# Streamed units of a second cross-attention: loads of turned weights placed behind other stores, query weights split earlier, two borders reordered

## The reference, cut to what matters

```python
q = (text_hidden @ Wq).reshape(B, T_text, N_HEADS, HEAD_DIM).transpose(0, 2, 1, 3)
...
scores = jnp.einsum('bhtd,bhsd->bhts', q, k) / scale
scores = jnp.where(mask, scores, -jnp.inf)
attn = jax.nn.softmax(scores, axis=-1)
out = jnp.einsum('bhts,bhsd->bhtd', attn, v)
out = out.transpose(0, 2, 1, 3).reshape(B, T_text, N_HEADS * HEAD_DIM)
return out @ Wo
```

## Time and profile before

| what | value |
|---|---|
| median of three runs | 2262.18 us |
| the profiled execution's own time | 2273.13 us |
| its span | 2271.1 us |
| TensorE busy | 2167.3 us, 95% |
| VectorE busy | 1467.5 us, 65% |
| ScalarE busy | 1051.5 us, 46% |
| GpSimd busy | 773.7 us, 34% |
| mean granted TensorE clock | 0.985 |
| streamed units, first to last turn | 878.6 to 1614.6 us |

### The profile page before, as it was taken

The page is one execution under the profiler, slowest core; times in us unless marked ns, Lnnn a source line. Parts: engine busy times, 40 slices in busy tenths (PEclk is TensorE's granted clock), DMA queues, the critical chain, the costliest instruction groups (busy, mean ns, idle before and its releaser), DMA issues. The chain is left out here.

```text
span 2271.1 us, 32392 instructions
## 1 busy us (share of the span) xinstructions
PE 2167.3 (95%) x10153; PEld 1764.7 (78%) x10153; DVE 1467.5 (65%) x2989; ACT 1051.5 (46%) x1895; POOL 773.7 (34%) x705
## 2 busy tenths in 40 slices
PE   8999999999999998898999999898899999999999
PEld 6778788889999876676777767676677888888887
DVE  7864365546777685677777777777677555555544
ACT  5532210114665665666666666666564323323221
POOL 4423445521111262444545445554332202121000
PEclk9999999999999999999999999999999999999999
DMA  6422221116778694666666666666402233232331
GB/s 225 137 99 68 77 60 33 33 63 249 277 262 291 224 314 157 194 187 186 197 190 194 194 192 194 194 203 194 139 1 84 84 97 103 100 128 72 109 116 52
DMA packets 250573, 339.17 MB, mean 149 GB/s; under 512 B 22048, under 2 KB 159776, under 8 KB 247648
## 3 DMA queue, kind: packets, MB, share of 16 engines
q1 hardware_dynamic: 242224, 310.75, 41.9%
q0 software_dynamic: 8240, 27.01, 4.6%
HBM read 234.12 MB, written 103.55 MB: 149 GB/s over the span
## 5 line engine op out<-in xcount | busy, mean ns | idle before, releaser
L2266 POOL TENSOR_TENSOR xa_late_hi<-late_rows,route_wv_hi 128x512 fp32r<-128x512 f32 x228 | 296.1, 1321 | 233.2 <-ACT route_wv_hi L2330 232.7
L2356 ACT ACTIVATE route_weights<-route_weights,xa_minus_max 128x512 f32<-128x512 f32 x256 | 184.1, 719 | 162.6 <-DVE xa_minus_max L2556 161.9
L2637 DVE STREAM_TRANSPOSE route_weights<-route_weights 128x512 f32<-128x512 f32 x228 | 160.0, 702 | 134.1 <-DMA xa_pt<-route_weights 131.4
L2556 DVE CUSTOM_DVE_ANT_0 route_weights<-xa_ps_s,route_mask_bias 128x512 f32<-128x512 f32 x252 | 172.2, 684 | 4.0 <-issue 2.5
L2330 ACT ACTIVATE route_wv_hi<-late_rows 128x512 fp32r<-128x512 f32 x228 | 130.7, 622 | 70.8 <-DMA late_rows<-xa_pt 69.8
L3299 ACT ACTIVATE ffn_silu<-ffn_ps_gate,late_scales 128x512 f32<-128x512 f32 x63 | 43.4, 689 | 247.6 <-PE ffn_ps_gate L92 247.6
L90 PE MATMUL xa_ps_s<-route_kv_hi,xa_q_hi 128*128 128x512 f32 x256 | 110.1, 430 | 35.4 <-DVE xa_minus_max L2556 34.5
L90 PE MATMUL xa_ps_p<-late_xT_hi,late_wq_hi 128*128 128x512 f32 (+1 forms) x264 | 111.7, 423 | 32.9 <-DVE late_wq_lo L2538 21.7
L1539 POOL DMA_INDIRECT route_rows<-moe_xn,route_slot_token x39 | 44.5, 1140 | 238.7 <-PE ex_ps_t L1832 182.3
L3105 DVE TENSOR_TENSOR route_kv_lo<-route_weights,route_kv_hi 128x1024 fp32r<-128x1024 f32 x42 | 53.7, 1278 | 101.6 <-ACT route_kv_hi L3100 101.6
L1092 ACT ACTIVATE moe_silu<-moe_ps_gate 128x512 f32<-128x512 f32 x44 | 26.2, 596 | 190.5 <-PE moe_ps_gate L92 190.4
(11 more groups left out here) (585 smaller groups left out, 6689.4 us busy)
## 6 DMA issues: line engine op xcount, KB each, us to landing
xa_pt<-route_weights SPq DMA_DIRECT2D x228, 256.0 KB
late_rows<-xa_pt SPq DMA_DIRECT2D x456, 128.0 KB, 2.7
route_weights<-in_ffn_w SPq DMA_DIRECT2D x64, 512.0 KB, 3.7
route_weights<-in_expert_w SPq DMA_DIRECT2D x12, 1408.0 KB
route_weights<-wd_folded SPq DMA_DIRECT2D x64, 256.0 KB, 2.7
ex_w_raw<-in_expert_w SPq DMA_DIRECT2D x10, 1408.0 KB
moe_y<-ex_y SPq DMA_DIRECT2D x39, 256.0 KB, 3.5
route_weights<-in_expert_w SPq DMA_DIRECT2D x12, 768.0 KB
```

What stands on the lines that cost most here:

```text
L2266: pool.tensor_tensor(lo, raw_part(half, two), f32(hi), ALU.subtract).then_inc(M.pt_ready, PART)
L2356: act.activation(prob[slot][:], prob[slot][:], ACT.Exp, bias=nmx[:, slot:slot + 1], scale=-1.0, accum_out=tot[:, slot:slot + 1]).then_inc( ...
L2556: dve.tensor_tensor_reduce(out=prob[slot][:], in0=psS[slot % 2][:], in1=mask_of(b, quarters), scale=-SCALE, scalar=3.4e38, op0=ALU.add, op ...
L2637: dve.transpose(blocked[tt % 2][:], prob[tt][:]).then_inc(M.blocks_turned, 1)
```

## The change

In the first unit of the first group and at the border behind unit 56 a few steps also change places. The DMAs and instructions stay the same in number; none is made larger or smaller.

```diff
@@ queue of SyncE
                         store(0)
+                        if which != "first" or ul > 0:
+                            load_turned((ul - 1) % 2, u - 1, 1)
                         store(1)
                         store(2)
+                        store(3)
                         if which == "first" and u == 0:
                             sp.wait_ge(R.xn_turned, NT)
                         load_turned(ul % 2, u, 0)
-                        store(3)
-                        load_turned(ul % 2, u, 1)
                         if h == 1:
                             next_kv(pair + 1, g, b + 1)
@@ behind the groups
                 END = (GROUPS - 1) * UNITS + 1
+                load_turned(0, END - 1, 1)
@@ ScalarE, streamed
                         exp(i + 3, 3)
+                        if ul in (UNITS - 3, UNITS - 2):
+                            act.wait_ge(M.proj_done, streamed_q(u - 1).n + 1)
+                            split_q(g + 1, ul - (UNITS - 3))
                         if before:
                             turned_half(u - 1, 1)
...
                         exp(i + 6, 2)
-                        if ul == UNITS - 3:
-                            act.wait_ge(M.proj_done, streamed_q(u - 1).n + 1)
-                            split_q(g + 1, 0)
-                        if ul == UNITS - 2:
-                            act.wait_ge(M.proj_done, streamed_q(u - 1).n + 1)
-                            split_q(g + 1, 1)
@@ ScalarE, border
                         beside((ul, -1))
+                        if ul == 1:
+                            proj_high(streamed_pv(u - 2), o_hi[out_buf(B - 1, 1)])
                         exp(i + 3, 3)
                         if ul == 1:
-                            proj_high(streamed_pv(u - 2), o_hi[out_buf(B - 1, 1)])
@@ VectorE, streamed
                         if which == "first" and ul == 0:
-                            stored(dve, KVS - 1)
+                            masked_max(i + 3, 3, b)
+                            normalise(i + 2, 2, halves(g, ul, 2))
...
-                        masked_max(i + 3, 3, b)
+                        if which != "first" or ul > 0:
+                            masked_max(i + 3, 3, b)
...
-                        normalise(i + 2, 2, halves(g, ul, 2))
+                        if which != "first" or ul > 0:
+                            normalise(i + 2, 2, halves(g, ul, 2))
                         turn_blocks(u, i, ul, 1, halves(g, ul, 1), before)
+                        if ul in (UNITS - 3, UNITS - 2):
+                            split_q(g + 1, ul - (UNITS - 3))
...
-                        if ul == UNITS - 3:
-                            split_q(g + 1, 0)
-                        if ul == UNITS - 2:
-                            split_q(g + 1, 1)
@@ VectorE, border
+                        if ul == 1:
+                            proj_low(streamed_pv(u - 2), ...)
                         masked_max(i + 3, 3, b, True)
                         beside((ul, -1))
                         normalise(i + 2, 2, halves(g, ul, 2))
                         if ul == 1:
-                            proj_low(streamed_pv(u - 2), ...)
...
-                            add_x(pair - 1, B - 1, 2)
-                            add_x(pair - 1, B - 1, 3)
                             proj_low(streamed_q(u), qh[1], ql[1])
                             proj_low(streamed_pv(u - 1), ...)
                             turned_low(i, 0)
                             turned_low(i + 1, 1)
+                            add_x(pair - 1, B - 1, 2)
+                            add_x(pair - 1, B - 1, 3)
@@ TensorE, border
                             scores(i + 5, 1, 0, nk, True)
-                            output(pair - 1, B - 1, 2)
                             bank_free(streamed_q(u))
                             query(streamed_q(u), qb, h, range(KC))
+                            streamed_weighted(u - 1, pair, b % 2)
+                            output(pair - 1, B - 1, 2)
                             output(pair - 1, B - 1, 3)
-                            streamed_weighted(u - 1, pair, b % 2)
```

More of the change, by code:

```diff
@@ L2717, in beside @@
                                 split_gate_up_lo(dve, G, L, 1)
+                        if ul == 1:
+                            proj_low(streamed_pv(u - 2), o_hi[out_buf(B - 1, 1)], o_lo[out_buf(B - 1, 1)])
                         masked_max(i + 3, 3, b, True)
@@ L2722, in body @@
                         if ul == 1:
-                            proj_low(streamed_pv(u - 2), o_hi[out_buf(B - 1, 1)], o_lo[out_buf(B - 1, 1)])
                             masked_max(i + 4, 0, nb, True)
```

## The result

The changed kernel takes **2339.38 us** (median of 3 runs, 2339.1 to 2340.39) where the kernel before took 2262.18: ratio 1.0336, 95% interval 1.0293 to 1.0379, so 3.4% slower. The prediction was 2318 us, slower, in a range of 2288 to 2362. The profiled execution took 2339.1 us.

The account below looks back on a forecast made before the run. The prediction took a chain of DRAM stores and loads, not TensorE, as the bound. Seven groups at +8.5 us gave +60, the border -4: +56 on the median 2262 made 2318 us, range 2288 to 2362.

Parts of the forecast that it names:

- the ring: Second attention: VectorE turns T3, T0', store S0', load LB, ScalarE copy HB, T3'; 12.3 us in `ul` 1, 5, 7.
- T3 to T0' to S0' to LB: VectorE turn to next unit's first turn, its store, then the load: 3.08, 0.73 and 0.56 us.
- LB to HB: From issue of the unit's second load to ScalarE's copy of it: 4.4 us, low end 4.05.
- HB to T3': From ScalarE's copy of the load through scaling and exponential to VectorE's next T3: 3.51 us.
- `ul` 0 and 4: Units with keys, values and 512 KB of weights ahead of S0': 15.9 us, including 0.6 for late landing.
- The query-weight split: Early split in `ul` 5 and 6: TensorE's 21.7 us of waiting go, but no time is gained.
- next_kv: Keys and values directly behind LA, waiting for GpSimd's lo of the values: costs nothing, margin 1 us.
- The border: Stretch behind unit 56, where TensorE waits 1.57 and 2.10 us for lo parts: -4 us, between -3 and -5.
- T2's wait for a store nearly gone: VectorE's wait at T2 for S0 to land: most of its 131.4 us go, returning as idle time before T3.
- the clock: Rival: more TensorE pauses lower its granted clock, +7 us a group, 2366 us; chance 0.18 together with longer queueing.
- The faster rival: TensorE's 53.8 us of waits are the price and the change removes them: 2208 to about 2235 us, chance 0.07.
- the cancelling one: Rival: gain and loss cancel, which needs all load landings below 3.4 us: 2262 us, chance 0.05.

Follow-up runs that it names:

- run 1: Kernel before with only the change's order of SyncE's queue, query weights split late and borders as before: 2351.94 us, ratio 1.0402.
- run 2: Changed kernel with only its queue order undone, so early query-weight split and both borders kept: 2257.29 us, ratio 0.9972.
- run 3: Changed kernel with keys, values and weights moved behind the next unit's S0 and LB: 2279.03 us, ratio 1.0069.
- run 4: Changed kernel with load LB issued in its own unit, behind S3 and LA: 2265.84 us, ratio 1.0008.
- run 6: Kernel before with only the early split of the query weights, loads and borders as before: 2258.09 us, ratio 0.9977.
- run 7: Kernel before with only the changes in the first unit and behind unit 56, loads and split as before: 2258.62 us, ratio 0.9973.
- run 8: Changed kernel with the old load order, but keys, values and weights behind the next unit's S0: 2243.31 us, ratio 0.9915.
- run 9: Changed kernel with the old load order, but keys and values behind the next unit's S0, weights behind its S1: 2220.02 us, ratio 0.9809.
- run 10: As run 9, but the weights behind S1 of `ul` 3 and 7, units without keys: 2211.54 us, ratio 0.977.

## Why the prediction was right

The direction, the mechanism and every link of the ring were right: runs 1 and 2 put the loss in the queue's order, runs 3 and 4 in its two links. The size was 21 us short, from one mis-sized term and one wrong step. Point by point:

- **T3 to T0' to S0' to LB**: 3.08, 0.73 and 0.56 us predicted, 3.07, 0.73 and 0.54 to 0.57 measured; 5.53 us at `ul` 2.
- **LB to HB** in plain units: 4.4 predicted, 4.15 to 4.2 measured (medians of `ul` 1, 5 and 7; 4.00 in the unit shown). That is nearer to the low end; before the change it was 4.1 in the same units, so standing right behind a store that is just issued cost under 0.1 us. An estimate by the Trainium skill (DMA: Bandwidth & Descriptors, Anatomy of one DMA) was 3.65; the trace is about 0.5 longer here too.
- **HB to T3'**: 3.51 predicted, 3.5 to 3.7 measured. Plain units 12.0 to 12.1 (predicted 12.3), `ul` 3 14.4 (14.7), `ul` 2 and 6 14.6 (14.3).
- **`ul` 0 and 4**: 15.9 predicted, medians 16.6 and 16.8. **This term was mis-sized**: "LB queues behind that S0, so it may lose 0 to 1.16 us; I take the middle, 0.6". LB to HB took 5.7 us in `ul` 0 and 6.5 in `ul` 4 (medians), 1.3 and 2.1 more than the 4.4, above the upper end of 1.16. The bound was read from T2 behind an S0 with LB, keys and weights ahead of it; now LB itself is issued 1.0 us behind the weights. Where the trace has the landing of such a weight load (`ul` 0), it comes 4.1 us after the issue (median), so the two overlap.
- **The sum**: 112.0 us a group predicted, 113.7 measured; +60 for the stretch, +71 measured. `ul` 0 and 4 are 1.6 us above the forecast together and `ul` 2 and 6 0.6; the plain units and `ul` 3 are 1.0 below, which hid part of it. The rest lies in single units slower than their medians.
- **The step from the profiled execution to the median** failed. The +56 was the forecast group less 103.5, the group of one execution 11 us above the median, and it was then added to the median. Runs 2, 6 and 7, with the loads in the old order, have groups of 102.3 to 102.4. In run 7, whose loads and split in this stretch are those of the kernel before, 103.5 less 102.4 is 8 us over seven groups: so most of the 11 us seems to have sat in this very stretch. No second execution of the kernel before was profiled to confirm it. Measured against 102.4 the forecast of 112.0 is 67 us, and with the border's -4 the time 2325. Of the 21 us that the forecast fell short, 8 come from this and 12 from the groups' own 1.7 us.
- **The query-weight split** at nothing: right in the group (runs 6 and 7), and right that it shortens T3 to T0' (run 1 without it, 4.56). **next_kv** at nothing: the keys were issued 3.30 us behind T3 (1162.98 less 1159.68), right behind LA. The **first unit** at nothing: T3 of unit 0 at 889.79 against 889.99. **The border** at -4: the tail fell by 5.0, and by 4.7 from run 1 to the changed kernel.
- "T2's wait for a store nearly gone" was wrong: 50.2 us of it are left, at T2 in units behind keys and weights. It lies beside the wait for HB and costs nothing, as argued.
- **The rivals**: the clock did fall, 0.97 to 0.94 in the stretch, and TensorE's busy time grew by 15 us with it. But the links of the ring have no TensorE in them and kept their lengths, so nothing is left for the clock that the landings behind the weights don't explain. The faster rival fell with run 6, and the cancelling one with the landings. The Trainium skill (Perfetto Trace Analysis, Identifying the Most-Contended Engine) would have had TensorE improved first. At 102 us a group the runs disagree: taking its 21 us of waiting for `late_wq_lo` away moved nothing. Whether the rule holds at 95 us a group no run tried.

## What to carry to other kernels

Follow one chain from an instruction to its successor in the next iteration before believing a busy share: a kernel with TensorE 95% busy was paced by a store, a load and the two engines that were busy 65% and 46%. In a queue that issues in order, a DMA's place is a dependency. Move a load behind a store only if the store's data is ready when the load would have gone, and put bulk loads behind the last transfer that somebody asks for soon, spread over the iterations that have none. Compare a forecast with several executions of the same stretch, not with the one that was profiled, before adding it to a median.

## What was not expected of the hardware

- Keys, values and weights, 0.5 MB and 0.5 MB, ahead of other transfers cost them more than the time of their issue: four 128 KB loads issued 1.0 us behind them had landed 5.7 to 6.5 us after their first issue instead of 4.1 (4.5 to 4.6 behind the keys and values without the weights), and a 256 KB store right behind them (run 8) 4.7 to 5.4 us after its issue, where behind the keys and values alone (run 9) it was 2.2 to 2.8.
- Four loads right behind four others (run 4) land 0.5 to 0.9 us later than four behind a single store (4.6 to 5.0 against 4.1 us).
- The same matmuls of the stretch took 676 us of TensorE's time at a granted clock of 0.94 and 634 at 0.99, in run 10, the kernel with fewer pauses: 43 us of its own busy time, beside the time of the pauses. That the pauses are the cause wasn't tried apart.
